# Routing scores formed batch by batch inside the local attention, on the projection banks

## The chip, the cores and the metric

The kernel runs on one core of a Trainium2 chip. TensorE multiplies matrices into PSUM; VectorE, ScalarE and GpSimd work on tiles; SyncE issues DMA. In the profile they are PE (PEld for its weight loads), DVE, ACT, POOL and SP. Each engine takes its own instructions in program order and waits on semaphores for the others. The metric is the time of one execution in device microseconds.

## The reference, cut to what matters

Two layers of attention and feed-forward work on x of 16 batches x 512 tokens x 128 channels. The change touches the first residual sum and the scores taken from it:

```python
x = x + _layernorm(_L0_attn_ref(_layernorm(x, axis=-1), ...), axis=-1)          # local attention, window 32
x = x + _layernorm(_L0_ffn_ref(_layernorm(x, axis=-1), ...), axis=-1)
# in _L0_ffn_ref:
feat = x.reshape(-1, D)                        # 8192 tokens x 128
norm = layer_norm(feat, ln_g, ln_b)
scores = norm @ centroids.T                    # 8192 x 8
sort_by_expert = balanced_assignment(scores)   # 8 times the 1024 best of the tokens left
```

## The kernel before

Five stages follow each other: `l0_attention`, `routing`, `expert_ffn`, `l1_attention`, `l1_ffn`. Only the first two are touched.

**Local attention.** A batch of 512 tokens (4 tiles of 128) is worked in 8 steps, one for each pair of heads; s is the step's number in its batch, n the number over all batches. Steps overlap by fixed lags, and all five engines run the same `program`: two batches written out, a loop over twelve, and the last two written out with a tail. In step s TensorE forms, in this order, q (L507), k (L507), in step 4 the transposes of the next batch's input (`xn`, L491), in even steps `rows`, the output projection of an earlier pair (L515), in odd steps the second half of the weighted values (L610), one tile of v (L499), then masks and scores (L545 to L588), and last the softmax sums (L601, odd steps) or the first half of the weighted values (L610, even steps).

The results of q, k, `xn` and v all go through two PSUM banks, `proj0` and `proj1`, which are used in turn. A use is freed when ScalarE has copied it out (semaphore `copied`); q and k are moreover read by VectorE for the rotary product (L444, semaphore `rope_done`), so the use after next of the same bank waits for that too. This is `bank_of`. A batch has 25 uses. Without `xn`, the use after q of the same bank is v, and TensorE does `rows` or L610 between k and v.

VectorE, in each step: the rotary product of q and of k (L444), in odd steps the normalisation L450, the row maxima of the scores of two steps ago (L460), the small statistics of the input, of the output and of the sum x1, then in odd steps a reciprocal of 128x512 (L476, once the sums L601 are there), in even steps the normalisation L481. The reciprocal of an odd step stands in the queue right ahead of the next even step's L444. GpSimd multiplies and adds the other half of the rotary product (L268, L273) and takes the powers -1/2. Work of a batch that isn't bound to a step is placed by numbers such as `SUM_Y` = 18 and `ROOT_SUM` = 19: step s of batch b + at//8, counted from the batch's own first step. After `ROOT_SUM` the mean and the factor 1/std of the sum x1 stand in SBUF.

**Routing.** It starts behind a barrier. Six loads come in, then 16 groups of 4 tiles pass a pipeline: VectorE normalises x1 (L883, `zz`), TensorE transposes (L827, `tp`), ScalarE applies gamma and beta (L803, `nT`), TensorE multiplies with the centroids (L817, `sp`), VectorE copies the 128x32 scores out (L874). Then VectorE turns the scores into integers (L895 on) and searches the eight thresholds, with a small matmul for each count.

## Time and profile before

| | us |
|---|---|
| median of 3 runs | 2756.76 (2747.97 to 2757.8) |
| profiled execution | 2750.51, span 2748.7 |
| first steps to the last projection of the local attention | about 23 to 1037 |
| end of the local attention's last factor | 1083.7 |
| score pipeline of the routing | 1085.15 to 1128.64 |
| threshold search and scatter | to about 1400 |

How to read it: a timeline's row is start, duration, engine, line, operation, output and inputs, and in brackets how long the engine was idle before and what ended that. Consecutive like instructions are merged (x16), so the start of the next row tells when the engine went on. [...]

### The profile page before, as it was taken

To read this page: it belongs to the slowest core of one execution; us is meant where nothing else is said; L and a number is where in the kernel's file an instruction comes from. 1 tells how busy PE (TensorE), PEld (TensorE's weight loads), DVE (VectorE), ACT (ScalarE), POOL (GpSimd) and SP (SyncE) were. 2 spreads that over 40 slices of the span, in tenths; PEclk is the share of its full clock that TensorE was granted. 3 is DMA by queue.
4 is the path that set the end of the run, shared out by engine and by line. 5 is a ranking of instruction groups with operands and counts; after the bars stand their busy time and mean duration, and the time that the engine had idled before them with its cause. 6 is when DMAs were issued, how large, how long until landed. Compare 5 with 4: busy or idle time off the path is not lost. (4 is left out here: it accounts for less than half of the span.)

```text
span 2748.7 us, 73587 instructions
## 1 busy us (share of the span) xinstructions
PE 2061.8 (75%) x26748; PEld 1195.5 (43%) x26748; DVE 1992.3 (72%) x5289; ACT 1552.3 (56%) x2872; POOL 1218.4 (44%) x1067
## 2 busy tenths in 40 slices
PE   5988989888988896411009928888888888888587
PEld 3776767676767675400004402232222322322354
DVE  4676767676777666688407817898888988987698
ACT  5665656565655563100004416787777777877587
POOL 5666666666667562000263357632432343230122
PEclk9999999999999998555559968999999999999799
DMA  4333333333333331000022232221112212220001
GB/s 115 75 79 72 71 77 74 75 80 72 79 76 75 71 73 25 1 0 0 19 64 76 81 70 49 51 41 27 25 32 34 33 26 31 35 32 2 13 23 35
DMA packets 103680, 136.73 MB, mean 50 GB/s; under 512 B 23781, under 2 KB 78981, under 8 KB 103046
## 3 DMA queue, kind: packets, MB, share of 16 engines
q1 hardware_dynamic: 99206, 123.34, 20.7%
q0 software_dynamic: 4096, 8.40, 1.1%
q8 instruction: 232, 3.80, 0.6%
q14 instruction: 146, 1.20, 0.2%
HBM read 26.52 MB, written 12.58 MB: 14 GB/s over the span
## 5 line engine op out<-in xcount | busy, mean ns | idle before, releaser
L1788 DVE TENSOR_REDUCE d_nmax_<-d_s_ 128x2 bf16<-128x1024 f32 x512 | 614.9, 1222 | 128.6 <-PE d_s_ L1950 126.9
L1699 ACT ACTIVATE d_pT_<-d_t_ 128x512 f32<-128x512 f32 x1024 | 558.2, 601 | 170.8 <-PE d_t_ L1962 163.3
L268 POOL TENSOR_TENSOR a_other<-a_other,a_rope 128x512 f32<-128x512 f32 x256 | 323.2, 1284 | 358.0 <-DMA a_other<-a_raw 357.2
L1975 PE MATMUL d_o_<-d_pT_,d_v_ 128*32 128x256 f32 x4096 | 326.3, 403 | 0.2 <-ACT d_pT_ L1699 0.2
L1962 PE MATMUL d_t_<-d_qs_,d_ks_ 49*128 49x512 bf16 x1024 | 207.7, 402 | 86.8 <-ACT d_pT_ L1699 41.6
L336 ACT ACTIVATE a_pT<-a_t 64x384 f32<-64x384 f32 x512 | 248.3, 485 | 19.2 <-PE a_t L588 7.5
L476 DVE RECIPROCAL a_rden<-a_o 128x512 f32<-128x512 f32 x64 | 214.7, 3355 | 49.5 <-PE a_o L601 49.4
L299 ACT COPY a_v<-a_proj 128x512 f32<-128x512 f32 x128 | 74.9, 585 | 278.8 <-PE a_proj L499 278.8
L460 DVE TENSOR_REDUCE a_nmax<-a_s 128x4 bf16<-128x384 f32 x256 | 130.7, 552 | 134.7 <-PE a_s L565 134.3
L1950 PE MATMUL d_s_<-d_ks_,d_qs_ 48*128 48x512 bf16 x1024 | 206.9, 400 | 17.5 <-DVE d_nmax_ L1788 12.1
L1155 ACT ACTIVATE c_hT_<-c_in_,c_beta_,c_gamma_ 128x512 f32<-128x512 f32 x16 | 12.4, 777 | 328.0 <-PE c_in_ L1275 328.0
L1962 PEld LDWEIGHTS d_t_<-d_qs_,d_ks_ 49*128 49x128 bf16 x1024 | 49.8, 93 | 316.7 <-ACT d_pT_ L1699 219.9
L790 POOL DMA_INDIRECT sorted_x<-x_tokens,pos x64 | 61.5, 962 | 283.0 <-DVEq L687 263.8
L317 ACT COPY a_raw<-a_proj 128x512 f32<-128x512 f32 x256 | 148.7, 586 | 60.7 <-PE a_proj L507 49.7
L610 PE MATMUL a_o<-a_pT,a_v 128*32 128x160 f32 (+1 forms) x4096 | 160.6, 296 | 12.7 <-DVE a_oT L481 9.5
L1975 PEld LDWEIGHTS d_o_<-d_pT_,d_v_ 128*32 128x32 f32 x4096 | 88.8, 110 | 183.2 <-ACT d_pT_ L1699 94.9
L273 POOL TENSOR_TENSOR a_kT<-a_kT,a_other 128x512 f32<-128x512 f32 x128 | 164.1, 1282 | 0.0
L273 POOL TENSOR_TENSOR a_qT<-a_qT,a_other 128x512 f32<-128x512 f32 x128 | 164.1, 1282 | 0.0
L844 PE MATMUL b_tot<-b_count,b_ones 128*128 128x3 bf16 x126 | 23.5, 186 | 170.5 <-DVE b_junk L926 158.7
L610 PEld LDWEIGHTS a_o<-a_pT,a_v 128*32 128x32 f32 x4096 | 120.1, 110 | 46.3 <-DVE a_oT L481 19.5
L515 PE MATMUL a_y<-a_wo,a_oT 128*128 128x128 f32 x1024 | 135.6, 290 | 0.8 <-DVE a_oT L450 0.8
L515 PEld LDWEIGHTS a_y<-a_wo,a_oT 128*128 128x128 f32 x1024 | 133.6, 206 | 5.9 <-DVE a_oT L450 1.1
(260 smaller groups left out, 4641.6 us busy)
## 6 DMA issues: line engine op xcount, KB each, us to landing
a_other<-a_raw SPq DMA_DIRECT2D x512, 128.0 KB, 2.3
d_qs_<-d_part_ SPq DMA_DIRECT2D x192, 64.0 KB
d_ks_<-d_part_ SPq DMA_DIRECT2D x192, 64.0 KB
a_xpre<-x SPq DMA_DIRECT2D x16, 256.0 KB, 3.8
a_xres<-x SPq DMA_DIRECT2D x16, 256.0 KB, 3.5
c_xs_<-sorted_x SPq DMA_DIRECT2D x16, 256.0 KB, 2.7
c_w_<-e_w SPq DMA_DIRECT2D x16, 256.0 KB, 3.3
sorted_x<-c_xs_ SPq DMA_DIRECT2D x16, 256.0 KB, 2.0
```

What stands on the lines that cost most here:

```text
L268: nc.gpsimd.tensor_tensor(other[s % 2][:, side, :], other[s % 2][:, side, :], rope[:, 1, :], ALU.mult).then_inc(rope2_done, 1)
L273: nc.gpsimd.tensor_tensor(dst, dst, other[s % 2][:, side, :], ALU.add).then_inc(add_done, 1)
L317: nc.scalar.copy(raw[s % 2][:, side, :], proj[bank][:, 0:T]).then_inc(copied, 1)
L336: nc.scalar.activation(dst[rows, :, 64 * c:64 * c + HB], src[rows], ACT.Exp, scale=SCALE).then_inc(exp_done, 1)
L476: nc.vector.reciprocal(rden[:], o_ps[:, 0:T]).then_inc(rden_done, 1)
L515: ins = nc.tensor.matmul(y_ps[:, t * 128:(t + 1) * 128], oT[:, 2 * (chunk % 2) + half, t * 128:(t + 1) * 128], wo_sb[:, 2 * chunk + half, ...
L610: ins = nc.tensor.matmul(o_ps[QD * i:QD * (i + 1), 128 * t:128 * t + widths[t]], v_sb[k_v][:, t, col:col + QD], pT[k_p][i][:, BAND * t:BAN ...
L1699: nc.scalar.activation(pT[kt][pair][:, a, :], t_bank(j, turn)[:], ACT.Exp).then_inc(t_read, 1)
L1788: nc.vector.reduce_max(out, s_bank(unit, e)[:], AX_X, negate=True).then_inc(s_read, 1)
L1950: nc.tensor.matmul(s_bank(unit, e)[:, a, :], qs[e.k][rows, hp, qt * 128:(qt + 1) * 128], ks[e.k][rows, hp, :], start=True, stop=True).then ...
L1962: nc.tensor.matmul(t_bank(2 * n + a, e)[:], ks[e.k][rows, hp, kt * 128:(kt + 1) * 128], qs[e.k][rows, hp, :], start=True, stop=True).then_ ...
L1975: ins = nc.tensor.matmul(o_ps[HC * i:HC * (i + 1), cols], v[e.k][:, kt, g * GH + i, :], pT[kt][i // 2][:, i % 2, cols], start=(kt, half) = ...
```

## The change

The score pipeline leaves `routing` and becomes three more tasks of each batch of the local attention: `NORM_SUM` = 20 on VectorE (normalise x1 of the batch into `zz`), `TURN_SUM` = 21 (four transposes into a projection bank, use "zn"; ScalarE writes `nT` with gamma and beta), and `SCORE` = 22 (four tiles times the centroids into a projection bank, use "sc"; ScalarE copies into `score`). For batch b these fall in steps 4, 5 and 6 of batch b + 2. A batch has 27 uses, and what held the same bank two uses back decides which semaphore is waited for (`use_two_back`). The tail becomes three steps longer. Three small loads move to the head of the local attention; the routing keeps two.

```diff
-        NLOADS = 4
+        NLOADS = 7
...
+        NORM_SUM, TURN_SUM, SCORE = 20, 21, 22
...
+            if s == TURN_SUM % PAIRS:
+                uses += [("zn", s)]
+            if s == SCORE % PAIRS:
+                uses += [("sc", s)]
             uses += [("v", s)]
...
-            for r in range(PAIRS + ROOT_SUM + 1):
+            for r in range(PAIRS + SCORE + 1):
...
@@ scalar, after xn and ahead of v
+                if s == TURN_SUM % PAIRS and formed(b, "zn", s):
+                    use, bank = use_of(b, k, s, "zn")
+                    act.wait_ge(proj_done, use + 1)
+                    nc.scalar.activation(nT[:], proj[bank][:, 0:T], ACT.Identity, bias=beta[:],
+                                         scale=gamma[:]).then_inc(copied, 1)
+                if s == SCORE % PAIRS and formed(b, "sc", s):
+                    use, bank = use_of(b, k, s, "sc")
+                    act.wait_ge(proj_done, use + 1)
+                    nc.scalar.copy(score[:, :, bass.ds(NT * (b - 2), NT)],
+                                   proj[bank][:, 0:NT * E].rearrange("p (t e) -> p e t", e=E)).then_inc(copied, 1)
...
@@ vector, behind the maxima, ahead of the reciprocal or L481
+            def sum_normalised(b):
+                dve.wait_ge(sum_step, b + 1)
+                for t in range(NT):
+                    ins = nc.vector.tensor_scalar(zz[:, t, :], x1[:, NT * b + t, :], mean[:, bass.ds(NT * b + t, 1)],
+                                                  comb1[:, bass.ds(NT * b + t, 1)], ALU.subtract, ALU.mult)
+                ins.then_inc(zz_ready, 1)
...
@@ tensor
-            def bank_of(b, k, s, what, before, left):
-                use, bank, odd = use_of(b, k, s, what, left)
-                pe.wait_ge(copied, use if odd else use - 1)
-                ready = {"q": 0, "k": None, "xn": 1, "v": 2 if s == TURN_X % PAIRS else 1}[what]
-                if ready is not None and (before or ready):
-                    pe.wait_ge(rope_done, 2 * (PAIRS * b + s) + ready)
+            def bank_of(b, k, s, what):
+
+                use, bank = use_of(b, k, s, what)
+                pe.wait_ge(copied, use - 1)
+                held = use_two_back(b, s, what)
+                if held[1] in ("q", "k"):
+                    pe.wait_ge(rope_done, 2 * (PAIRS * held[0] + held[2]) + 1 + (held[1] == "k"))
                 return bank
...
+                if s == TURN_SUM % PAIRS and formed(b, "zn", s):
+                    bank = bank_of(b, k, s, "zn")
+                    pe.wait_ge(zz_ready, b - 1)
+                    for t in range(NT):
+                        ins = nc.tensor.transpose(proj[bank][:, t * 128:(t + 1) * 128], zz[:, t, :], ident[:])
+                    ins.then_inc(proj_done, 1)
+                if s == SCORE % PAIRS and formed(b, "sc", s):
+                    bank = bank_of(b, k, s, "sc")
+                    turned_use, _ = use_of(b, k, TURN_SUM % PAIRS, "zn")
+                    pe.wait_ge(copied, turned_use + 1)
+                    for t in range(NT):
+                        ins = nc.tensor.matmul(proj[bank][:, t * E:(t + 1) * E], nT[:, t * 128:(t + 1) * 128], cent[:],
+                                               start=True, stop=True)
+                    ins.then_inc(proj_done, 1)
                 if s % 2 == 0 and alive(LAG_ROWS, before, left):
...
@@ routing
-            groups(dve, one)
-            for m in range(GROUPS - 2, GROUPS):
-                kept(m, m % 2)
-            dve.wait_ge(sc_kept, GROUPS)
             bits = score[:].bitcast(I32)
```

TensorE in step 6 of a batch in the loop, in the kernel before: the three passes of k, then the output projection, then v. Names with `a_` are the local attention's tiles.

```order
L507 MATMUL a_proj<-a_xnT_hi,a_w_lo 128x512 [waits a_copied]
L507 MATMUL a_proj<-a_xnT_lo,a_w_hi 128x512
L507 MATMUL a_proj<-a_xnT_hi,a_w_hi 128x512
L633 REGISTER_ALU
L515 MATMUL a_y<-a_wo,a_oT 128x128 [waits a_norm_done]
L515 MATMUL a_y<-a_wo,a_oT 128x128 x7
L523 REGISTER_ALU
L526 REGISTER_ALU [waits a_copied]
L499 MATMUL a_proj<-a_w_lo,a_xnT_hi 128x512 [waits a_xnT_ready,a_rope_done]
```

The same place in the changed kernel (its k is L558, the output projection L566, v L550):

```order
L558 MATMUL a_proj<-a_xnT_hi,a_w_lo 128x512 [waits a_copied]
L558 MATMUL a_proj<-a_xnT_lo,a_w_hi 128x512
L558 MATMUL a_proj<-a_xnT_hi,a_w_hi 128x512
L575 REGISTER_ALU
L578 ISA [waits a_copied]
L694 MATMUL a_proj<-a_cent,a_nT 128x8 [waits a_copied,a_rope_done]
L694 MATMUL a_proj<-a_cent,a_nT 128x8 x3
L699 REGISTER_ALU
L566 MATMUL a_y<-a_wo,a_oT 128x128 [waits a_norm_done]
L566 MATMUL a_y<-a_wo,a_oT 128x128 x7
L575 REGISTER_ALU
L578 REGISTER_ALU [waits a_copied]
```

The wait for the rotary product of q (`a_rope_done`) now stands ahead of the output projection, with the score matmuls; it stood behind it, at v.

TensorE in step 5, before:

```order
L507 MATMUL a_proj<-a_xnT_hi,a_w_hi 128x512
L639 REGISTER_ALU
L610 MATMUL a_o<-a_pT,a_v 32x160 [waits a_norm_done]
L610 MATMUL a_o<-a_pT,a_v 32x160 x11
L610 MATMUL a_o<-a_pT,a_v 32x128 x4
```

And in the changed kernel:

```order
L558 MATMUL a_proj<-a_xnT_hi,a_w_hi 128x512
L575 REGISTER_ALU
L578 ISA [waits a_copied]
L687 MATMUL a_proj<-a_ident,a_zz 128x128 [waits a_zz_ready,a_rope_done]
L687 MATMUL a_proj<-a_ident,a_zz 128x128 x3
L705 REGISTER_ALU
L662 MATMUL a_o<-a_pT,a_v 32x160 [waits a_norm_done]
L662 MATMUL a_o<-a_pT,a_v 32x160 x11
```

Here too a wait for `a_rope_done` and four transposes have come between k and the weighted values.

## Rows read from the trace of the kernel before

**Rows 1.** The page, the clock granted to TensorE in 40 slices of the span.
```profile
PEclk9999999999999998555559968999999999999799
```

**Rows 2.** Busy time by engine in stretches: start:end, length, busy and count, clock, DMA.
```profile
core 0: us, PE busy (x) PEld busy (x) DVE busy (x) ACT busy (x) POOL busy (x), PEclk, DMA share, GB/s
...
108.20:1047.00 938.80, 833.88 (x16639) 657.67 (x16638) 665.82 (x1220) 568.34 (x1083) 616.83 (x503) 0.98 0.32 75
...
448.81:456.90 8.09, 7.34 (x140) 6.03 (x136) 5.52 (x5) 4.82 (x10) 6.57 (x6) 1.00 0.38 93
...
1085.15:1128.64 43.49, 39.90 (x192) 39.40 (x192) 20.75 (x83) 12.43 (x16) 0.00 (x0) 0.50 0.02 3
```

**Rows 3.** Timeline of TensorE in step 6: last pass of k, rows, v.
```profile
450.08 0.39 PE L507 MATMUL a_proj<-a_xnT_hi,a_w_hi 128*128 128x512 f32 x1
450.31 1.95 PE L515 MATMUL a_y<-a_wo,a_oT 128*128 128x128 f32 x16
453.00 0.50 PE L499 MATMUL a_proj<-a_w_lo,a_xnT_hi 128*128 128x512 f32 x1 [0.75 <-DVE a_qT L444]
```

**Rows 4.** Timeline of VectorE, the same step.
```profile
449.04 3.36 DVE L476 RECIPROCAL a_rden<-a_o 128x512 f32<-128x512 f32 x1 [1.64 <-PE a_o L601]
452.32 0.63 DVE L444 TENSOR_TENSOR a_qT<-a_proj,a_rope 128x512 f32<-128x512 f32 x1
```

**Rows 5.** Timeline of TensorE in a step 4, from the xn transposes to v.
```profile
630.23 0.65 PE L491 MATMUL a_proj<-a_ident,a_xpre 128*128 128x128 f32 x4 [2.60 <-DVE a_qT L444]
630.72 1.95 PE L515 MATMUL a_y<-a_wo,a_oT 128*128 128x128 f32 x16
632.42 0.48 PE L499 MATMUL a_proj<-a_w_lo,a_xnT_hi 128*128 128x512 f32 x1
```

**Rows 6.** Stretches, TensorE alone: a step 3 with its step 4, twice.
```profile
core 0: us, PE busy (x), PEclk, DMA share, GB/s
...
422.26:430.45 8.19, 6.73 (x156) 1.00 0.30 67
...
430.45:442.15 11.70, 9.10 (x143) 0.85 0.21 48
...
619.30:625.97 6.67, 6.67 (x156) 1.00 0.36 84
...
625.97:636.30 10.33, 7.73 (x144) 1.00 0.23 52
```

**Rows 7.** Timeline of TensorE in step 5: last pass of k, weighted values.
```profile
443.42 0.40 PE L507 MATMUL a_proj<-a_xnT_hi,a_w_hi 128*128 128x512 f32 x1
443.74 1.24 PE L610 MATMUL a_o<-a_pT,a_v 128*32 128x160 f32 x32
```

**Rows 8.** Timeline of VectorE in step 5.
```profile
443.76 0.69 DVE L444 TENSOR_TENSOR a_qT<-a_proj,a_rope 128x512 f32<-128x512 f32 x1 [0.78 <-ACT a_raw L317]
```

**Rows 9.** Timelines of GpSimd and of VectorE at the end of step 4.
```profile
440.63 1.28 POOL L273 TENSOR_TENSOR a_kT<-a_kT,a_other 128x512 f32<-128x512 f32 x1
...
442.29 0.69 DVE L481 TENSOR_TENSOR a_oT<-a_o,a_rden 128x512 f32<-128x512 f32 x1 [1.55 <-PE a_o L610]
```

**Rows 10.** Timeline of all engines in the routing's score pipeline.
```profile
1085.15 2.14 DVE L883 TENSOR_SCALAR b_zz<-x_tokens,mean,comb 128x128 f32<-128x128 f32 x8
...
1109.35 1.09 PE L827 MATMUL b_tp<-b_ident,b_zz 128*128 128x128 f32 x4
...
1110.23 1.72 PE L817 MATMUL b_sp<-b_cent,b_nT 128*128 128x8 f32 x8
...
1110.48 0.78 ACT L803 ACTIVATE b_nT<-b_tp,b_beta,b_gamma 128x512 f32<-128x512 f32 x1 [1.60 <-PE b_tp L827]
1111.61 0.88 PEld L827 LDWEIGHTS b_tp<-b_ident,b_zz 128*128 128x128 f32 x4
1111.80 1.09 PE L827 MATMUL b_tp<-b_ident,b_zz 128*128 128x128 f32 x4
...
1128.64 0.43 DVE L895 TENSOR_SCALAR b_sign<-b_score 128x512 int32<-128x512 int32 x1
```

**Rows 11.** Timeline of TensorE, its first matmul that waits for all loads.
```profile
17.04 0.77 PE L499 MATMUL a_proj<-a_w_lo,a_xnT_hi 128*128 128x512 f32 x1 [7.46 <-DVE a_w_lo L393]
```

More of the change, by code:

```diff
@@ L159, in l0_attention, with formed, use_of, use_two_back @@
                 uses += [("xn", s)]
+            if s == TURN_SUM % PAIRS:
+                uses += [("zn", s)]
+            if s == SCORE % PAIRS:
+                uses += [("sc", s)]
             uses += [("v", s)]
         HEAD_USES = 1 + V_AHEAD
-        def formed(what, s, left):
+        assert TURN_SUM // PAIRS == SCORE // PAIRS == 2 and len(uses) % 2 == 1
+        def formed(b, what, s):
+            if not isinstance(b, int):
+                return True
             if what == "xn":
-                return left > PAIRS
+                return b + 1 < NB
             if what == "v":
-                return left > PAIRS if s >= V_FIRST else left > 0
-            return left > 0
-        def use_of(b, k, s, what, left):
-            u = uses.index((what, s))
-            last = left + s <= PAIRS
-            out = [w for w in uses[:u] if not formed(w[0], w[1], left + s - w[1])] if last else []
-            return HEAD_USES + len(uses) * b + u - len(out), (HEAD_USES + u + k) % 2, bool(out)
+                return b + (s >= V_FIRST) < NB
+            if what in ("zn", "sc"):
+                return 2 <= b < NB + 2
+            return b < NB
+        numbered = [(b, what, s) for b in range(NB + 2) for what, s in uses if formed(b, what, s)]
+        LEFT_OUT = 2 * sum(what in ("zn", "sc") for what, _ in uses)
+        def use_of(b, k, s, what):
+            if isinstance(b, int):
+                number = HEAD_USES + numbered.index((b, what, s))
+                return number, number % 2
+            u = uses.index((what, s))
+            return HEAD_USES + len(uses) * b + u - LEFT_OUT, (HEAD_USES + u + k) % 2
+        def use_two_back(b, s, what):
+            if isinstance(b, int):
+                at = numbered.index((b, what, s))
+                return numbered[at - 2] if at >= 2 else (0, "v", 0)
+            u = uses.index((what, s)) - 2
+            return b + u // len(uses), *uses[u]
         def v_unit(b, k, s):
@@ L314, in projected @@
                 for side, what in enumerate("qk"):
-                    use, bank, _ = use_of(b, k, s, what, left)
+                    use, bank = use_of(b, k, s, what)
                     act.wait_ge(proj_done, use + 1)
@@ L441, in step @@
                     for side, (what, dst) in enumerate((("q", qT[s % 4]), ("k", kT[s % 4]))):
-                        use, bank, _ = use_of(b, k, s, what, left)
+                        use, bank = use_of(b, k, s, what)
                         dve.wait_ge(copied, use + 1)
@@ L626, in step @@
                     for side, what in enumerate("qk"):
-                        bank = bank_of(b, k, s, what, before, left)
+                        bank = bank_of(b, k, s, what)
                         project(k, s, side, bank)
-                if s == TURN_X % PAIRS and formed("xn", s, left):
-                    transposes(b + 1, bank_of(b, k, s, "xn", before, left))
+                if s == TURN_X % PAIRS and formed(b, "xn", s):
+                    transposes(b + 1, bank_of(b, k, s, "xn"))
+                if s == TURN_SUM % PAIRS and formed(b, "zn", s):
[12 more added lines that the diff above has]
+                    ins.then_inc(proj_done, 1)
                 if s % 2 == 0 and alive(LAG_ROWS, before, left):
@@ L668, in _, with routing @@
             program(pe, step)
-def routing(nc, x1, pos, mean, comb, cent_t, ln_g, ln_b, ident_in, ones_in, before_in, sorted_x):
+def routing(nc, x1, pos, score, ones_in, before_in, sorted_x):
     _, TILES, C = x1.shape
-    E = cent_t.shape[1]
+    E = score.shape[1]
     CAP = TILES * 128 // E
-    G4 = 4
     DIGITS = 8
@@ L734, in routing @@
         one_col = sb("one_col", [128, TILES])
-        tp = [ps(f"tp{k}", [128, 512]) for k in range(2)]
-        sp_ps = [ps(f"sp{k}", [128, 512]) for k in range(2)]
         tot = ps("tot", [128, 512])
@@ L754, in routing @@
         scattered = sem("scattered")
-        NLOADS = 6
+        NLOADS = 2
         CNT = 2 * DIGITS + 2
-        GROUPS = TILES // G4
-        def groups(engine, one):
-            for m in range(4):
-                one(m, m % 2)
-            with engine.Fori(2, GROUPS // 2) as i:
-                for k in range(2):
-                    one(2 * i + k, k)
-        def at_least(m, n):
-            return not isinstance(m, int) or m >= n
         block = ctx.enter_context(nc.Block())
@@ L2387, in program @@
         rstd = ctx.enter_context(nc.sbuf_tensor("rstd", [128, TILES], F32))
+        score = ctx.enter_context(nc.sbuf_tensor("score", [128, a["centroids"].shape[1], TILES], F32))
         l0_attention(nc, a["x"], a["l0_w"], a["l0_wo"], a["l0_rope"], a["l0_masks_q"], a["l0_masks_k"], a["ident"], x,
[L2389 to L2390 removed]
+                     mean, comb, a["centroids"], a["ln_g"], a["ln_b"], score)
+        routing(nc, x, pos, score, a["ones"], a["before"], sorted_x)
         expert_ffn(nc, sorted_x, a["e_w1"], a["e_b1"], a["e_w2"], a["e_b2"], a["ln_g"], a["ln_b"], a["ident"], sorted_x2)
```

94 lines of the change are left out of this document (23 added, 71 removed).

## The prediction, made before the changed kernel ran

> **What bounds the kernel now.** I read the granted clock of the page first, then busy time by stretches, then the timelines of single steps. The slices show two regimes: full clock up to slice 15, half clock through the routing [rows 1]. In the local attention TensorE is busy 833.9 of 938.8 us, 89%, and VectorE 71%, ScalarE 61%, GpSimd 66% [rows 2]: TensorE carries the stage, and what is added to its queue, work or wait, is added to the stage unless one of its remaining waits shrinks. The timeline shows where these are. An even step without `xn` takes 8.09 us [rows 2]: behind k come the rows, then TensorE waits 0.75 us for the rotary product of q before v may take the bank [rows 3]. That product is late in even steps, since the reciprocal of 3.36 us stands ahead of it on VectorE: 449.04 + 3.36 = 452.40, product to 452.95, v at 453.00 [rows 3, 4]. So the end of TensorE's sums (which starts the reciprocal) to v is a fixed chain of some 4.2 us, and q, k and the rows are hidden in it. In the routing the score pipeline is bounded by TensorE's records at half clock: 39.9 us busy of 43.49 [rows 2].
>
> **The gain.** The score pipeline goes from the routing. Its first instruction on VectorE starts at 1085.15, the first one behind it at 1128.64 [rows 10]: 43.5 us. I expect the conversion to start at 1085.2 instead. The two loads that stay are needed by the first count only, some 4 us later (the conversion is six passes of about the 0.43 us of its first row and more [rows 10]), and no longer by the first transposes, so nothing comes in for the gain.
>
> **The tail.** The last batch has its factors just before the barrier and now must pass the three tasks alone. By the rows of the pipeline at half clock: `zz` 2.14 / 2 = 1.1; transposes to `nT` 1110.48 - 1109.35 = 1.1; `nT` 0.78; matmuls 1.7; the copy and five hand-overs, which I can only bound between 0.2 and 1.2 (nothing but the copy of a 128x32 tile, or as much again as `nT` with half a microsecond for the hand-overs), and take as 0.7 [rows 10]. Sum 5.4 us, bounds 4.9 to 5.9. The other batch that falls in the tail meets an idle TensorE. Left of the gain: 43.5 - 5.4 = 38.1 us.
>
> **Step 6, the score matmuls.** They stand between k and the rows, and wait for the rotary product of q. That is what `xn` does in step 4 already, the nearest row: there TensorE waits 2.60 us at the transposes, and v follows the rows without a wait [rows 5]; the step takes 10.33 us at full clock against 8.09 for step 6 now, 2.24 more [rows 2, 6]. The rows are pushed out of the shadow of the reciprocal. In place of the four transposes, which hold TensorE for 630.72 - 630.23 = 0.49 us, come eight records of the score matmuls. At half clock eight hold it for 1111.80 - 1110.23 = 1.57 us, so 0.79 at full clock, if it halves; sixteen records of the rows (the same weights' size) take 632.42 - 630.72 = 1.70, so 0.85 for eight [rows 5, 10]. I take 0.85. Step 6: 2.24 + 0.85 - 0.49 = 2.6 us at full clock. I see nothing of it given back later in the batch, since the next waits of TensorE (step 0, 2, 3) are for VectorE work that starts from TensorE's own sums and moves with them.
>
> **Step 5, the transposes of x1.** VectorE has no reciprocal ahead of q here. It starts the product of q at 443.76, since ScalarE's copy ends then, and ends at 444.45; `xn` starts about 0.1 us behind such an end, so 444.55. TensorE would be ready at 443.74 [rows 7, 8]: a wait of 0.8, and 0.5 for the transposes at full clock, 1.3 us. The weighted values and v come later by that, and the rotary product of k, which v now waits for and which follows q's at once (445.15, if it takes as long), is past. Bounds: 0.5, if the product were no wait, and 2.2, the transposes at half clock (1.0) and a late VectorE.
>
> **The clock.** In each batch the wait of step 4 may be followed by a fall to half. Of fourteen windows of step 4 eight have a granted clock of 1.00 and take 10.2 to 10.3 us, six have 0.78 to 0.86; five of these take 11.7 to 12.2, some 1.6 us more [rows 6]. The six falls are all among the eight batches whose step 3 had a wait too (longer than 7 us against 6.7), and none among the six without. In the changed kernel step 6 has a wait of 2.6 us with one of 0.8 in the step ahead in each batch, like these eight. I take 0.7 falls of 1.6 us a batch, 1.1 us; bounds 0 and 1.8 (each time, and a bit at step 5). [...] The trace agrees that waits matter, and shows that not each one does [rows 6].
>
> **VectorE, ScalarE, GpSimd, loads: nothing.** The four `zz` instructions (1.1 us) go between the maxima, done at 442.29 - 1.55 = 440.74, and L481, which waits for TensorE until 442.29; they fit by 0.4 us [rows 9]. If GpSimd's addition, which runs to 441.91, holds them up, they end at 443.0, L481 at 443.7, and the product of q at 443.76 is still in time. ScalarE's `nT` (0.78) and the score copy come ahead of v's copy, which waits for TensorE anyway; behind them are v's copy, the casts and the exponentials, all later by the same as v. The `copied` that the score matmuls want is 5 us old by then. The three loads at the head come in while TensorE waits until 17.04 for the split weights [rows 11]; if that cover were gone they would cost 1.4 us once. No DMA is moved past another one in the loop, and SP's and POOL's order is unchanged but for these.
>
> **The sum.** A batch costs 1.3 + 2.6 + 1.1 = 5.0 us. Fourteen batches (0 to 13) have their tasks while TensorE is loaded: 70 us. Net 70 - 38.1 = +32 us. Against the profiled execution of 2750.5 that is 2783, against the median of 2756.8 it is 2789. The three runs lie 10 us apart, so I take a value between, **2787 us**. With no falls of the clock and 3.9 a batch it is +16.5, 2767 to 2773; with the upper bounds (2.2 + 2.6 + 1.8 = 6.6 a batch) +54, 2805 to 2811.
>
> **The rivals.**
>
> *Hidden after all, faster.* Only TensorE's own time counts, 0.49 + 0.85 = 1.3 us a batch, because the waits that the new uses take are the ones that v took (0.75 in even steps) and what is pushed out is caught up at the waits of steps 2 and 3. Then 14 x 1.3 - 38.1 = -19 us, 2732 to 2738. The point from which it decides: below 38.1 / 14 = 2.7 us a batch the kernel is faster. For it: TensorE does wait 11% of the stage [rows 2]. Against: in step 4 the same arrangement costs 2.24 us in each of its undisturbed windows, more than its transposes, and isn't caught up in step 5 [rows 5, 6]. Chance 0.07.
>
> *Nearly even.* Step 5's product of q is in time and the clock doesn't fall: 0.5 + 2.6 = 3.1 a batch, 43.5 - 38.1 = +5, about 2756 to 2762. For it: eight of fourteen step 4 show no fall. Against: ScalarE's copy of q can't start before TensorE is done with q, and that chain is longer than k. Chance 0.13.
>
> *Far slower.* `zz` on VectorE is held up by more than one GpSimd instruction of 1.28 us, L481 and then the product of q come late, and TensorE, which waits for it in step 5, waits 1.3 us more: 14 x 1.3 = 18 us on top, 2801 to 2807, and with a fall of the clock each time 2810. For it: the fit is 0.4 us, and GpSimd works on kT just then [rows 9]. [...] Against: GpSimd is idle from 441.91 on, so there is one instruction to wait out, not two. Chance 0.10.
>
> **How the numbers follow.** Forecast (+16 to +54) 0.70, far slower 0.10, even 0.13, faster 0.07. The range leaves out the fast rival and the far end: 2758 to 2808. Of the forecast's 0.70 I put 0.01 within 0.5%, at its lower end. A measurement tells 0.5% (14 us, so 2743 to 2770.5) from no change: slower by more 0.79, within 0.14, faster 0.07.
>
> **What would show it.** In the profile after: the score matmuls of step 6 wait about 2.6 us for the product of q, and v follows the rows without a wait; that step takes 10.7 at full clock, 12.3 with a fall; step 5 goes from 6.66 to 8.0 with a wait of 0.8 at the transposes; the last projection of the attention is some 70 us later; the conversion starts 1.5 us behind the barrier. It would be wrong if the undisturbed step 6 took under 9.5 us, if the wait of step 5 were gone, or if other steps grew.

## The result and the profile after

The changed kernel takes **2835.09 us** (median of 4 runs, 2831.83 to 2840.82) against 2757.28 (2747.97 to 2758.72) for the one before, run beside it: a ratio of **1.0303**, 95% interval 1.0275 to 1.0331. I predicted slower, 2787 us, with a range to 2808; it is slower by 2.4 times the +32 us of my sum. The profiled execution has a span of 2829.6 us, 80.9 more than before.

From the timelines the span divides like this (us):

| stage | before | after | difference | predicted |
|---|---|---|---|---|
| to the first projection of v | 17.0 | 20.3 | +3.3 | 0 |
| step 5 of the batches | 108.1 | 130.5 | +22.4 | +18.2 |
| step 6 | 128.4 | 196.3 | +67.9 | +51.8 with the falls |
| steps 7 and 0 | 236.8 | 248.8 | +12.0 | 0 |
| steps 1 to 4 | 528.7 | 513.7 | -15.0 | 0 |
| rest of the attention | | | +0.7 | 0 |
| last factors to the conversion | 44.9 | 6.6 | -38.3 | -38.1 |
| conversion to the first scatter | 218.9 | 247.1 | +28.2 | 0 |
| first scatter to the end | 1401.2 | 1400.9 | -0.3 | 0 |

The step sums leave out steps 0 to 2 of the first batch, which stand in "rest of the attention". The clock by slices answers [rows 1]; no stage of it changes level (a fall within one step lasts 3.4 or 6.8 us and is too short to show in a slice of 71 us). The granted clock is a share of full speed, 1.00 or, in a fall and through the routing, 0.50. Then the stretches of after (columns as in [rows 2]): the attention, the search, and the stage behind.

```profile
PEclk9999999999999999755556986999999999999899
```

```profile
core 0: us, PE busy (x) PEld busy (x) DVE busy (x) ACT busy (x) POOL busy (x), PEclk, DMA share, GB/s
108.20:1130.00 1021.80, 885.41 (x16658) 701.87 (x16658) 687.35 (x1263) 579.11 (x1105) 617.12 (x505) 0.94 0.29 69
...
1181.64:1428.70 247.06, 27.93 (x156) 15.18 (x156) 178.93 (x1418) 0.00 (x0) 0.00 (x1) 0.50 0.01 1
1428.70:2829.60 1400.90, 1066.76 (x8032) 411.27 (x8032) 1047.28 (x2384) 905.86 (x1653) 527.58 (x491) 0.90 0.20 39
```

The last two of them in the kernel before:

```profile
1128.64:1347.50 218.86, 27.78 (x156) 15.02 (x156) 178.28 (x1415) 0.00 (x0) 0.00 (x0) 0.50 0.00 0
1347.50:2748.70 1401.20, 1065.08 (x8032) 410.73 (x8032) 1045.88 (x2384) 904.61 (x1653) 526.11 (x491) 0.90 0.20 39
```

VectorE is as busy in the search as before (178.9 and 178.3 us) and the search takes 28.2 us longer: the engine stood idle.

**Step 6**, TensorE, in the batch at 479.26; compare [rows 3, 5]. Behind k it waits 2.53 us, then come the scores, the rows and v, without a wait of v. The four score matmuls stand there as 8 records and the eight of the rows as 16, while each pass of k and of v, with its fp32r halves, is one:

```profile
480.52 0.40 PE L558 MATMUL a_proj<-a_xnT_hi,a_w_hi 128*128 128x512 f32 x1
483.45 1.06 PE L694 MATMUL a_proj<-a_cent,a_nT 128*128 128x8 f32 x8 [2.53 <-DVE a_qT L493]
484.36 3.37 PE L566 MATMUL a_y<-a_wo,a_oT 128*128 128x128 f32 x16
487.38 0.77 PE L550 MATMUL a_proj<-a_w_lo,a_xnT_hi 128*128 128x512 f32 x1
```

The rows take 3.37 us, where [rows 3, 5] have 1.95 at the full clock; the clock granted from 484.40 to 487.40 is 0.57. In other batches the scores are slow too, as here in the batch before, with 0.53 granted in the scores (406.20 to 408.00) and 0.50 in the rows (408.00 to 411.50):

```profile
406.30 1.88 PE L694 MATMUL a_proj<-a_cent,a_nT 128*128 128x8 f32 x8 [2.53 <-DVE a_qT L493]
408.02 3.76 PE L566 MATMUL a_y<-a_wo,a_oT 128*128 128x128 f32 x16
```

The windows of these two steps and of a step 5 (start:end, length, TensorE busy, granted clock):

```profile
core 0: us, PE busy (x), PEclk, DMA share, GB/s
402.11:416.04 13.93, 11.40 (x148) 0.75 0.17 39
...
471.24:479.26 8.02, 7.32 (x159) 1.00 0.35 83
479.26:491.64 12.38, 9.85 (x147) 0.86 0.23 56
```

Of the fourteen batches seven have a step 6 of 12.38 to 12.40 us, five one of 13.93 to 13.95, and the last two 12.25 and 11.59. None of the fourteen is at full clock throughout: their granted clock is 0.75 to 0.86. Two more profiles hold the same order: in pad21 below all fourteen fell, in zz_other thirteen; the fourteenth waited the same 2.53 us, kept 1.00 and took 10.77 us.

**Step 5.** TensorE first (compare [rows 7]), then VectorE and GpSimd in another batch, in which TensorE waits 1.17 us at the transposes:

```profile
472.50 0.40 PE L558 MATMUL a_proj<-a_xnT_hi,a_w_hi 128*128 128x512 f32 x1
473.60 0.66 PE L687 MATMUL a_proj<-a_ident,a_zz 128*128 128x128 f32 x4 [0.70 <-DVE a_qT L493]
```

```profile
681.97 3.07 DVE L481 TENSOR_SCALAR a_zz<-x_tokens,mean,comb 128x128 f32 x4
684.96 0.68 DVE L532 TENSOR_TENSOR a_oT<-a_o,a_rden 128x512 f32<-128x512 f32 x1
685.56 0.67 DVE L493 TENSOR_TENSOR a_qT<-a_proj,a_rope 128x512 f32<-128x512 f32 x1
```

```profile
682.16 1.29 POOL L305 TENSOR_TENSOR a_qT<-a_qT,a_other 128x512 f32<-128x512 f32 x1
683.40 1.29 POOL L305 TENSOR_TENSOR a_kT<-a_kT,a_other 128x512 f32<-128x512 f32 x1
```

`zz` takes 1.11 us in the tail, with GpSimd idle, and 3.07 here beside two GpSimd instructions, so that the product of q ends at 686.23. In the first twelve of the fourteen batches step 5 takes 8.0 to 8.1 us where `zz` took 1.9 to 2.7 us, and 8.25 to 8.6 where it took 2.8 to 3.2.

**The tail**, all engines (compare [rows 10]):

```profile
1175.02 1.11 DVE L481 TENSOR_SCALAR a_zz<-x_tokens,mean,comb 128x128 f32<-128x128 f32 x4 [1.12 <-POOL comb L286]
...
1176.28 1.09 PE L687 MATMUL a_proj<-a_ident,a_zz 128*128 128x128 f32 x4 [9.19 <-DVE a_zz L481]
1177.41 0.78 ACT L381 ACTIVATE a_nT<-a_proj,a_beta,a_gamma 128x512 f32<-128x512 f32 x1 [9.70 <-PE a_proj L687]
...
1178.33 1.85 PE L694 MATMUL a_proj<-a_cent,a_nT 128*128 128x8 f32 x8 [0.96 <-ACT a_nT L381]
1180.21 0.19 ACT L386 COPY score<-a_proj 128x32 f32<-128x32 f32 x1 [2.03 <-PE a_proj L694]
```

From 1175.02 to the end of the copy are 5.4 us, and the conversion starts at 1181.64.

**The search.** VectorE's timeline at one jump back of the loop over the experts (line 957 is the last of the body, 934 the first), then its waits over the whole search (engine, tile, line, releaser: sum, times, longest):

```profile
1215.01 0.14 DVE L957 TENSOR_SCALAR b_base<-b_base 128x1 f32<-128x1 f32 x1
1218.47 0.23 DVE L934 TENSOR_TENSOR b_a<-b_hi,b_free 128x64 f32<-128x64 f32 x1 [3.31 <-issue]
...
1220.73 0.09 DVE L900 DVE_READ_ACCUMULATOR b_junk<-b_a,b_tries 128x1 bf16 x1 [1.51 <-issue]
```

```profile
DVE b_a L934 <- issue: 19.0, 6, 3.3
DVE b_junk L900 <- issue: 9.1, 6, 1.6
```

Before, the first line of the body waits for VectorE's own last result, 3.1 us in six times. The two gaps make 19.0 + 9.1 - 3.1 = 25.0 of the 28.2 us; where the other 3.2 stand was not traced. "Issue" is time in which the engine waited for nothing that the profile shows. The profile's list of DMA queues (queue, packets, MB, share) has one more difference, before and after:

```profile
q14 instruction: 146, 1.20, 0.2%
```

```profile
q14 instruction: 175, 1.43, 0.2%
```

That is 29 packets of code more, about five for each of the six jumps back. That the queue is VectorE's is inferred: it follows the place of VectorE's loop in every kernel here. This queue has 175 packets in every kernel below that has the gaps, and 146 or 121 in those without.

**The head.** Four small operations that normalise the first rows take 5.21 us (1.98 before) beside GpSimd's memsets, which stand there in both kernels, and the first matmul that waits for all loads comes later than [rows 11]:

```profile
6.40 5.21 DVE L423 TENSOR_SCALAR a_xpre<-a_xpre,a_mv,a_comb 128x128 f32<-128x128 f32 x4 [1.21 <-POOL a_comb L282]
```

```profile
20.31 0.76 PE L550 MATMUL a_proj<-a_w_lo,a_xnT_hi 128*128 128x512 f32 x1 [7.46 <-DVE a_w_lo L435]
```

It isn't the change's: an unchanged copy of the kernel before had it at 20.2, and the changed kernel with 21 memsets, none of them at the head, at 17.1.

### The profile page after: what moved, and what is told of

It is laid out like the page before. It is cut to its first block and busy times, and to the rows that moved or that the text cites. A ratio compares the mean times of both kernels' runs of the same rounds, so it can differ in the third digit from the quotient of the medians.

```text
span 2829.6 us, 73415 instructions
## 1 busy us (share of the span) xinstructions
PE 2085.5 (74%) x26748; PEld 1209.6 (43%) x26748; DVE 2003.5 (71%) x5273; ACT 1557.1 (55%) x2888; POOL 1217.7 (43%) x1067
## 5 line engine op out<-in xcount | busy, mean ns | idle before, releaser
L368 ACT ACTIVATE a_pT<-a_t 64x384 f32<-64x384 f32 x512 | 248.8, 486 | 20.5 <-PE a_t L640 8.8
L662 PE MATMUL a_o<-a_pT,a_v 128*32 128x160 f32 (+1 forms) x4096 | 160.3, 295 | 10.3 <-DVE a_oT L532 7.1
L566 PE MATMUL a_y<-a_wo,a_oT 128*128 128x128 f32 x1024 | 159.1, 321 | 0.0
L566 PEld LDWEIGHTS a_y<-a_wo,a_oT 128*128 128x128 f32 x1024 | 154.8, 235 | 4.0 <-issue 0.6
L662 PEld LDWEIGHTS a_o<-a_pT,a_v 128*32 128x32 f32 x4096 | 120.0, 109 | 40.4 <-DVE a_oT L532 17.9
```

What stands on the lines that cost most here:

```text
L368: nc.scalar.activation(dst[rows, :, 64 * c:64 * c + HB], src[rows], ACT.Exp, scale=SCALE).then_inc(exp_done, 1)
L566: ins = nc.tensor.matmul(y_ps[:, t * 128:(t + 1) * 128], oT[:, 2 * (chunk % 2) + half, t * 128:(t + 1) * 128], wo_sb[:, 2 * chunk + half, ...
L662: ins = nc.tensor.matmul(o_ps[QD * i:QD * (i + 1), 128 * t:128 * t + widths[t]], v_sb[k_v][:, t, col:col + QD], pT[k_p][i][:, BAND * t:BAN ...
```

## Experiments

The ratios are to the kernel before, run on the same chip each time. On those chips before took 2752 to 2775 us, so only ratios and stages are compared. Where a run is called lower or higher by less than 2%, its interval is what tells it from 1.

**Where the search's loop lies.** VectorE's loop ends at instruction 1069 of its built program before, at 1048 after. Theory A is that the place of the loop's code alone makes the search slower, 247.1 us against 218.9, by gaps of some 3.2 and 1.5 us at each of six jumps back. First, 21 memsets put it back:

```diff
             program(dve, step)
+            for j in range(21):
+                nc.vector.memset(blank[:, j:j + 1], 0.0)
```

> The changed kernel with 21 more memsets of one column each on VectorE, at the end of the local attention, where VectorE waits for the barrier (about 4 us idle). They bring the body of the threshold search back to the place in VectorE's instruction stream that it had in the kernel before (first instruction 850 in place of 829). [...] It expects the search at 219 us, the two gaps of each round gone, and 28 us less in all, about 2807. Rival, the data: the search is slower since the scores, now written by ScalarE in another stage, or the missing loads, change what it waits for. It expects 247 us still and 2835. [...]

Measured: ratio 1.0201 (1.0157 to 1.0244), the search 219.0 us, both kinds of gap gone, the queue's packets back at 146. Steps 5 and 6 are unchanged (129.9 and 197.7 us). Twenty-one instructions of no use make the kernel 1% faster, and 1% is the search's 28 us. The converse, 40 memsets in the kernel before (the loop then ends at 1109):

> The kernel before with 40 such memsets on VectorE at the end of the local attention: its search loop moves from 850..1069 to 890..1109. [...] The rival expects no change in the search, 2757.

Measured: ratio 1.0041 (1.0011 to 1.007), the search 218.8 us, no gaps. By theory A I had expected the gaps of the changed kernel at this place too, with a search of some 247 us and 28 us more in all, about 2785, and that missed: the first line of the body waits 0.51 to 0.55 us at the six jumps back, as in before (0.51 to 0.54). So not every other place costs. The body of 220 built instructions leaves 286 records in each turn, since each of 66 reductions with an accumulator leaves two. In this run the packets of code went to 121, 25 fewer than in before, and the search took no less for it: the packets by themselves are no price. The sharper experiment puts before's loop exactly where the changed kernel has it, from 829 to 1048. By theory A the gaps then stand in it too, the search takes 247 us and the ratio is 1.010:

```diff
@@ vector, semaphore steps_set declared ahead
-            for d in range(DIGITS):
-                for k in range(TIES):
-                    nc.vector.memset(steps[:, d, k:k + 1], float((k + 1) * 4 ** d))
+            for k in range(TIES):
+                nc.vector.memset(steps[:, 0, k:k + 1], float(k + 1))
+            dve.wait_ge(steps_set, TIES * (DIGITS - 1))
@@ gpsimd
+            for d in range(1, DIGITS):
+                for k in range(TIES):
+                    nc.gpsimd.memset(steps[:, d, k:k + 1], float((k + 1) * 4 ** d)).then_inc(steps_set, 1)
```

> The kernel before, with 21 of the 24 small VectorE memsets ahead of the threshold search made by GpSimd instead, so that the search's loop begins at the same place of VectorE's program as in the changed kernel (its last instruction is number 1048 of the built program, where before has 1069 and the changed kernel 1048). Nothing else of the change is in it. [...] Theory B (the gaps belong to something else that the change brings, and the runs with 21 and 40 memsets more fit by chance): no gap, 219 us, ratio 1.000.

Measured: ratio 1.0147 (1.0103 to 1.0192), the search 247.3 us, and the packets of its code queue 175. The line that begins the body is 964 in this kernel:

```profile
DVE b_a L964 <- issue: 19.3, 6, 3.3
DVE b_junk L930 <- issue: 9.0, 6, 1.5
```

So the place alone makes the 28 us, without anything of the change. The search itself is +28.4 us; as a whole the run is 13 us over the 1.010, which the interval just leaves out. Up to 3.3 us of that are the head, which was the late one in this profile, and the rest is not explained. The gaps and the 175 packets stand here and in the changed kernel, with the loop from 829 to 1048, and neither stands in before, pad21 (850) or before_pad40 (890). Why that place costs is not shown.

**Steps 6 and 5: which order costs.** In `late_sc` the scores stand behind the rows, ahead of v:

```diff
                 if s % 2 == 0 and alive(LAG_ROWS, before, left):
                     rows(quad, chunk)
+                if s == SCORE % PAIRS and formed(b, "sc", s):
+                    bank = bank_of(b, k, s, "sc")
...
+                    ins.then_inc(proj_done, 1)
                 if formed(b, "v", s):
```

> The changed kernel with the score matmuls of step 6 behind the rows, ahead of v. Theory B, the order: the wait for the rotary product isn't new, it only pushes the rows out of its shadow. It expects step 6 at 8.1 + 0.85 = 9.0 us without a fall of the clock, in place of 12.4 to 13.95: 14 x 4 = 55 us less, about 2780. Rival, the clock alone: the score matmuls (few columns) and any wait make the clock fall wherever they stand; then step 6 keeps 10.5 or more and the gain is under 30 us.

Measured: ratio 1.0140 (1.0095 to 1.0185). Step 6 takes 8.98 us in the steady batches, and the attention's last factors come 54.4 us earlier than in the changed kernel, where I had expected 55. The ratio fell by less, 0.016 (45 us). TensorE:

```profile
326.79 1.95 PE L566 MATMUL a_y<-a_wo,a_oT 128*128 128x128 f32 x16
329.48 1.06 PE L704 MATMUL a_proj<-a_cent,a_nT 128*128 128x8 f32 x8 [0.75 <-DVE a_qT L493]
330.39 0.48 PE L550 MATMUL a_proj<-a_w_lo,a_xnT_hi 128*128 128x512 f32 x1
```

The wait is the 0.75 us that v had before [rows 3]; the rows are in the shadow of the reciprocal again, at the full clock. What remains of the score operations is 0.9 us a step. `late_both` moves the transposes of step 5 behind the weighted values as well, in the same way:

> As late_sc, and the transposes of step 5 behind the weighted values, ahead of v. Theory B expects no wait at the transposes, step 5 at 6.66 + 0.5 = 7.2 in place of 8.0 to 8.6, another 14 x 1.2 = 17 us less, about 2763. Were the 0.7 to 1.3 us of step 5 of another cause than the order, it would stay at 2780.

Measured: ratio 1.0091 (1.0056 to 1.0125). Step 5 sums to 118.0 us instead of 132.4; seven of the fourteen steps take 7.04 us, where the weighted values fill the wait, and the others 7.2 to 8.4.

**Does the wait bring the clock down?** `filled` keeps the changed order and gives TensorE something to do in the wait:

```diff
+                if s == SCORE % PAIRS and formed(b, "sc", s) and (not isinstance(b, int) or b < NB):
+                    for _ in range(10):
+                        nc.tensor.matmul(y_ps[:], identb[:], zeros[:], start=False, stop=True, skip_group_check=True)
                 if s == SCORE % PAIRS and formed(b, "sc", s):
```

> The changed kernel with ten TensorE operations of 128x512 on a tile of zeros, added to the sum of the projection of the output, ahead of the score operations in step 6 of every batch; at the full clock ten take about 2.1 us, some four fifths of the 2.53 us wait. Theory (the wait of 2.53 us after that of step 5 is what makes the granted clock fall in step 6 of every batch): with the engine busy through it the clock stays up in most batches, step 6 takes 10.7 to 11.0 us instead of 12.4 to 13.95, 14 batches give back 25 to 40 us, and the ratio to before is 1.016 to 1.021. Rival (the clock is down for what step 4 or 5 did, or for the chip's own reasons): the ten take 4.3 us at half the clock, longer than the wait, step 6 takes 14 to 16 us and the ratio is 1.035 to 1.045. The search stage stays at 247 us by either.

Measured: step 6 takes 10.76 or 10.77 us in twelve batches, 10.68 and 9.99 in the last two, and its sum is 165.9 us instead of 196.3. TensorE and the window of one step (the granted clock is the column behind the busy time):

```profile
328.73 2.33 PE L693 MATMUL a_y<-a_zeros,a_identb 128*128 128x512 bf16 x10
331.41 1.06 PE L699 MATMUL a_proj<-a_cent,a_nT 128*128 128x8 f32 x8 [0.35 <-DVE a_qT L495]
```

```profile
327.22:337.99 10.77, 10.42 (x157) 1.00 0.22 50
```

The granted clock stays at 1.00 in all fourteen. So the idle time of 2.53 us is what brings it to 0.50 in this step, and it did so in 14 batches of 14, for 196.3 - 165.9 = 30.4 us. It is not enough by itself: the wait of 2.60 us in step 4 [rows 5] brought a fall in seven of these fourteen batches of the changed kernel, and what decides there is open. As a whole the run gives a ratio of 1.0282 (1.0239 to 1.0325), above what I expected: its step 5 and step 2 were 14 us longer than the changed kernel's, and the attention gained 18. By the time alone it can't be told from the changed kernel.

**Both cures together**, late_both with the 21 memsets:

> The changed kernel with the score operations behind the rows and the transposes behind the weighted values (as in late_both), and the 21 memsets of pad21. Both cures are expected to add: late_both was at 1.0091 of before with a search stage of 246 us; without the search's gaps 28 us less, so the stage at 219 us and a ratio of 0.999 (0.996 to 1.002): the change then costs nothing and gains nothing. Rival (the two overlap somewhere, or the stage behind the scatter differs): 1.005 or more.

Measured: ratio 0.9957 (0.9936 to 0.9978), the search 218.9 us. So the change can be had with a gain of 0.4% at most: the interval still touches that of an unchanged copy of before below (0.9963 to 1.001).

**The same cure for the transposes of step 4**, which wait 2.60 us in the kernel before already [rows 5]. In `late_all_pad`, on top of the above, they go behind the rows:

```diff
-                if s == TURN_X % PAIRS and formed(b, "xn", s):
-                    transposes(b + 1, bank_of(b, k, s, "xn"))
...
                     rows(quad, chunk)
+                if s == TURN_X % PAIRS and formed(b, "xn", s):
+                    transposes(b + 1, bank_of(b, k, s, "xn"))
```

> late_both_pad with the transposes of the next batch's normalised rows in step 4, which wait in every batch in the kernel before as well, also moved behind that step's rows. If what was learnt of steps 5 and 6 holds for step 4 (a wait of 2 to 2.5 us ahead of the rows, and a fall of the clock behind it in about half the batches), step 4 loses 2.2 us without and 3.9 us with a fall, some 45 us in 15 batches: ratio 0.983 (0.978 to 0.990). Rival (the next batch's first step needs those rows at once, so that the wait only moves): step 4 shorter but steps 5 to 7 longer by the same, ratio 0.997 to 1.000.

Measured: ratio 0.9908 (0.9877 to 0.9939), short of the 0.983 that I expected. Step 4 sums to 144.2 us instead of 182.1, but step 5 to 142.2 instead of 116.2. The reason stands on VectorE, with TensorE behind it:

```profile
368.28 4.89 DVE L482 TENSOR_SCALAR a_zz<-x_tokens,mean,comb 128x128 f32 x4 [0.24 <-POOL comb L287]
373.09 0.68 DVE L533 TENSOR_TENSOR a_oT<-a_o,a_rden 128x512 f32<-128x512 f32 x1
```

```profile
373.82 1.24 PE L665 MATMUL a_o<-a_pT,a_v 128*32 128x160 f32 x32 [2.71 <-DVE a_oT L533]
```

GpSimd ran four instructions, of 1.3 us each, from 368.10 to 373.09, and `zz` ended 0.08 us behind the last. That is the pattern throughout: every single `zz` operation that took over 0.6 us, 48 of 64 here and 23 of 64 in the changed kernel, ends 0.08 or 0.09 us behind the end of a GpSimd operation. I asked whether another form of the operation is spared:

```diff
-                    ins = nc.vector.tensor_scalar(zz[:, t, :], x1[:, NT * b + t, :], mean[:, bass.ds(NT * b + t, 1)],
-                                                  comb1[:, bass.ds(NT * b + t, 1)], ALU.subtract, ALU.mult)
+                    ins = nc.vector.scalar_tensor_tensor(zz[:, t, :], x1[:, NT * b + t, :], mean[:, bass.ds(NT * b + t, 1)],
+                                                         comb1[:, bass.ds(NT * b + t, 1)].to_broadcast([128, C]),
+                                                         ALU.subtract, ALU.mult)
```

> The changed kernel with its four normalising operations of a batch in another form, a scalar_tensor_tensor whose second operand is the factor repeated along the row, where they are a tensor_scalar with two operands a row. In the changed kernel they take 1.86 us beside one GpSimd operation and 3.07 beside two (1.11 in the tail, where GpSimd is idle), 37.3 us in 14 batches. Theory (the tensor_scalar is held up by GpSimd, as an operation with two full inputs, 0.68 us for 128x512 in every place, is not): the four take 1.0 to 1.3 us in every batch, the wait ahead of the transposes in step 5 is 0.70 us in all batches instead of 0.70 to 1.29, step 5 sums to 125 to 127 us instead of 130.5, and the time is 4 us less than the changed kernel, ratio 1.029. Rival (the length comes from something else): unchanged sums.

> late_all_pad with the same other form of the four normalising operations. There they take 58.0 us in 14 batches, 4.89 us in one of them beside four GpSimd operations, the weighted values of step 5 wait up to 3.1 us for the next VectorE operation, and step 5 sums to 142.2 us against 116.2 in late_both_pad. Theory (GpSimd holds up the tensor_scalar): they take 1.0 to 1.3 us, step 5 sums to 116 to 120 us, 22 to 26 us are gained over late_all_pad's ratio of 0.9908, and the ratio is 0.982 to 0.984. Rival (step 5 waits because the rotary products of q and k come late since the transposes moved): step 5 stays at 138 us or more, ratio 0.990.

Measured: ratios 1.0318 (1.0261 to 1.0375) and 0.9945 (0.9916 to 0.9974); `zz` took 36.0 and 57.5 us in 14 batches, as long as in the old form (37.3 and 58.0). The form is no cure, and these two runs did not tell the theories apart. A third took three of the four operations away:

```diff
-                for t in range(NT):
+                for t in range(1):
```

> late_all_pad with one of the four normalising operations of a batch left out for three of four tiles (those tiles' scores are formed from zeros), and 24 memsets more at the end, so that the search's loop keeps its place. In late_all_pad the four take 58.0 us in 14 batches, each as long as the GpSimd instruction that it meets (about 1.3 us), and 1.1 us for all four where GpSimd is idle. Theory (this length keeps the next operation of VectorE, and with it TensorE, waiting in step 5): one takes at most 1.4 us, step 5 sums to 116 to 120 us instead of 142.2, and the ratio is 0.980 to 0.984 against 0.9908. Rival (the rotary products of q and k come late since the transposes moved): step 5 stays at 138 us or more, ratio 0.990.

Measured: ratio 0.9834 (0.9799 to 0.9868), step 5 sums to 112.4 us, 7.03 to 7.05 in all fourteen batches. The scores of three tiles in four are no longer those of the reference in this kernel. With the order and the rotary products as they were, the length of `zz` behind GpSimd was what step 5 waited for.

**The kernel before with only that reordering.** First an unchanged copy, as a measure:

> The kernel before, unchanged, as a run of its own: it shows what two equal kernels differ by here, and gives a trace of before on this chip, since the stages behind the first scatter took 1410 to 1441 us in the profiles of the last two sets of runs against 1401.2 in the trace of before. Expected: ratio 1.000 within 0.003, the search stage 218.9 us; if the stage behind the scatter takes 1410 us or more here too, its length belongs to the chip, and if it takes 1401 us, the changed kernels carry a cost in it that is not found yet.

Measured: ratio 0.9986 (0.9963 to 1.001). Its stage behind the scatter takes 1422.5 us, 21 more than in before, so a difference of that size in this stage is not an edit's. The other profiles have 1404 to 1441 us there; that the ones above 1422.5 are of the same kind is likely, since no edit touches the code, but not shown. Then `before_late_xn`, the diff of late_all_pad's transposes alone, on the kernel before:

> The kernel before with one order changed: in step 4 of a batch the four transposes of the next batch's normalised rows stand behind that step's rows, where they stood ahead of them with a wait (as in late_all_pad, but without the routing scores). In late_all_pad against late_both_pad step 4 lost 37.9 us in sum and step 5 gained 26.0 us by waits for the normalised weighted values. Theory (the same here): step 4 loses about 38 us, step 5 gains up to 26 us, ratio 0.991 to 0.996. Rival (step 5 is free here, since no transposes of the sum stand in it): the whole 38 us stay, ratio 0.984 to 0.988.

Measured: ratio **0.9865** (0.984 to 0.9891), 2728.41 us. Step 4 sums to 141.9 us against 178.4 in the copy, and step 5 stays at 108.1, which is what the rival of the expectation said. TensorE in step 4, and its window:

```profile
348.97 1.95 PE L515 MATMUL a_y<-a_wo,a_oT 128*128 128x128 f32 x16
351.74 0.65 PE L491 MATMUL a_proj<-a_ident,a_xpre 128*128 128x128 f32 x4 [0.82 <-DVE a_qT L444]
```

```profile
347.48:356.17 8.69, 7.87 (x144) 1.00 0.27 62
```

Without `zz` nothing of it is lost again. This is faster than both kernels, and late_all_pad, which has this order and the change, stands at 0.9908. The intervals of the two touch (0.9891 and 0.9877), so with this order nothing here shows a gain of the change itself.

**TensorE's own jump back.** Steps 7 and 0 sum to 236.8 to 244.1 us in five profiles of kernels with before's loop where it was, and to 246.5 to 251.0 in profiles with the changed one. The two ends of the first range are two profiles of one kernel, before and its copy, and differ in step 0 (119.8 and 126.8 us; 126.1 in the changed kernel). The part that goes with the change is step 7, where the loop jumps back five times: TensorE's waits there, before and after (sum, times, longest).

```profile
PE a_proj L507 <- issue: 16.7, 5, 3.9
```

```profile
PE a_proj L558 <- issue: 22.3, 5, 4.7
```

```diff
             pe.wait_ge(const_set, 4)
+            for _ in range(256):
+                pe.wait_ge(const_set, 4)
```

> The kernel before with 128 instructions more in TensorE's program ahead of the loop over the batches (waits that are met already), so that the loop's code lies elsewhere. In before step 7 takes 10.0 us at the five jumps back against 6.66 otherwise, in the changed kernel 11.3. Theory (the jump back costs TensorE by the place of its code, as the search's does VectorE): steps 7 and 0 in sum, 236.8 us in before and 242.4 in the run with less memsets, move by over 6 us, up or down. Rival (the cost does not depend on the place, and the changed kernel's is due to its longer loop or to its waits): 236 to 243 us. The first projection comes up to 10 us later by either.

> late_all_pad with the same 128 instructions more ahead of TensorE's loop. Theory (place): steps 7 and 0, 246.5 us in late_all_pad, move by over 6 us, and by the same amount and sign as in before_pe128 if the start of the loop decides. Rival (length of the loop, or its waits): 245 to 249 us and step 7 at 10.8 to 11.3 us at the jumps back. Ratio 0.991 by the rival, and 0.987 to 0.995 by the theory.

Measured: steps 7 and 0 take 244.7 us in before_pe128, just above what before has anyway, and 238.1 in late_all_pe128, 8.4 less than late_all_pad. The five waits make 16.8 us there against 21.6 in late_all_pad, and step 7 is at 9.8 to 10.3 us instead of 10.8 to 11.3 at the jumps back. So the changed loop's 5.6 us more at the jumps (22.3 - 16.7) go with the place of its code. The other 6 of the +12 are step 0's, which the copy of before has too. That the move makes no less of the waits in before_pe128 (17.9 us) speaks against a simple rule. Both kernels paid for it in step 2 (without the first batch's): 148.0 and 151.9 us against 125 to 139 in the other profiles, by waits for a late product of q; late_all_pe128 also in step 5 (152.8 against 142.2). The times were 2788.38 us against 2770.38 for before (a single run) and a ratio of 1.0047 (1.002 to 1.0074). Why these steps react is open.

## Why the prediction was wrong

**The sign and the frame held.** The gain of the score pipeline (-38.3 against -38.1), the tail (5.4 us, as summed), the conversion's start and the stage behind were right. The two waits stand where I put them: 2.53 us at the scores (2.6 foretold) and 0.70 at the transposes (0.8). An undisturbed step 6 takes 10.77 us in `filled` (10.7 foretold), and step 5 with a short `zz` 8.02 (8.0). The last projection of the attention came 90 us later where I had said 70.

**The clock's term was mis-sized.** I took 0.7 falls a batch of 1.6 us, 1.1 us, with 1.8 as the upper bound. Measured are 14 falls in 14 batches, by 30.4 / 14 = 2.2 us each. I counted from [rows 6] that falls came only among step 4's with a wait in the step ahead, six of eight, and then weighed them as a chance; and I took five like windows for the size. That count was one trace's: in the changed kernel six of seven falls of step 4 came without such a wait, and in the copy of before seven of ten. In five batches the fall came early enough to slow the scores too and cost 3.2 us in place of 1.6. A fall of 1.6 us in every batch, which my upper bound allowed, would have been nearer than my 0.7 and makes the forecast +39.

**"VectorE: nothing" was too low.** The rival in which `zz` is held up by more than one GpSimd instruction had the right cause, at a smaller price than the 1.3 us a batch it named. Where `zz` meets two GpSimd instructions it takes 3.07 us and the product of q comes 0.47 us later; that is most of the 4.2 us by which step 5 exceeds the forecast. I looked at one window of GpSimd and let one instruction stand for all batches. The trace has the mark of it: each `zz` operation that was held up, 23 of 64 in the changed kernel, ends within 0.09 us of the end of a GpSimd instruction.

**The step that failed most was one that I did not write: the sum has no term for the search.** No operation of it changed, and I costed only operations. The change in the code ahead of it moved the loop by 21 instructions, from 850 to 829, for +28.2 us, nearly as much as my whole net sum. The built program has the shift, and I put it to no use. TensorE's loop is a smaller case of the same (+5.6).

**What remained in the sum.** 32 (net) + 14.7 (falls, 30.4 - 15.7) + 5.3 (steps 5 and 6 else) + 12.0 (steps 7 and 0, of which 5.6 at the jumps back) + 28.2 (search) + 3.3 (head) - 15.0 (steps 1 to 4) + 0.4 (rounding, the attention's rest) = 80.9. The -15 is mostly not the change's: the profile of before has two odd steps 2, of 14.84 and 12.25 us, and its copy none (127.3 us in sum, as after). My own mark for "wrong", that other steps grew, was met by steps 7 and 0.

## What to carry to other kernels

A task that must wait goes behind the work that needs no wait: the same operations ahead of the rows cost 4.9 us a batch and behind them 0.9, since the waiting task pushes out work that was hidden, and the idle time of 2.53 us took the clock down to 0.50 in 14 batches of 14. Before adding code, look where loops that follow it begin; the search's, of 286 records a turn, cost 4.2 us more at each jump back by its place alone (3.2 + 1.5 against 0.5), so test with a handful of idle instructions before blaming an operation. A VectorE operation like `zz`, which took 0.28 us alone and up to 1.3 us beside a busy GpSimd in the changed kernel, should be priced by GpSimd's instructions (1.3 us each), not by its own length. And a pattern counted in one trace, as that of the falls in step 4, wants a second trace of the same kernel before it goes into a sum.

## What the runs showed of the hardware

- A jump back of VectorE's loop of 220 built instructions costs 0.5 us at one place (before) and 3.2 + 1.5 us at another, 21 instructions earlier; the packets of its code queue go from 146 to 175 (121 at a third place, with no gap).
- Ten 128x512 bf16 operations in a 2.5 us wait kept the granted clock at 1.00 in all 14 batches (filled); without them it fell to 0.50 in 14 of 14, in 14 of 14 and in 13 of 14 batches of three kernels (the changed one, pad21, zz_other). Waits of 0.70 to 0.75 us at the scores behind the rows (late_sc) brought no fall in 14 batches.
- A `zz` of 128x128 (1.11 / 4 = 0.28 us alone) that meets a GpSimd instruction ends 0.08 to 0.09 us behind it (0.15 in the other form) and takes up to 1.3 us in the changed kernel (1.5 in late_both_pad); `a_oT`, one of whose inputs lies in PSUM, takes 0.67 to 0.69 us in every profile.
- The stage behind the scatter, whose code no edit touches, took 1401 to 1441 us in the profiles, and 1401.2 and 1422.5 in two of one kernel: a difference larger than most effects looked for here, so stages were compared one by one.
